# Self-attention stage with float16 value weights, DMA-placed low parts and one interleaved order for all units

## The reference

```python
xn = layernorm(x)
q, k, v = (einsum('ntc,hdc->nhtd', xn, w) for w in (w_q, w_k, w_v))
a = einsum('nhtd,nhsd->nhts', q, k) / 8
a = where(col > row, -inf, a)              # causal
y = einsum('nhts,nhsd->nthd', softmax(a), v)
x = x + y.reshape(8, 512, 1024) @ w_o
```

## Time and profile before

| what | value |
|---|---|
| median of 3 runs | 2338.05 us (2337.87 to 2339.3) |
| profiled execution, its own time | 2323.5 us |
| its span, first to last instruction | 2321.0 us |
| busy over the span: array, VectorE, ScalarE, GpSimd | 1981.3, 1371.9, 1193.5, 697.6 us |
| self-attention stage in the span | from the start to about 1023 us |

### The profile page before, as it was taken

The page is one execution under the profiler, slowest core; times in us unless marked ns, Lnnn a source line. Parts: engine busy times, 40 slices in busy tenths (PEclk is TensorE's granted clock), DMA queues, the critical chain, the costliest instruction groups (busy, mean ns, idle before and its releaser), DMA issues. The chain is left out here.

```text
span 2321.0 us, 38463 instructions
## 1 busy us (share of the span) xinstructions
PE 1981.3 (85%) x13976; PEld 1030.2 (44%) x13976; DVE 1371.9 (59%) x2614; ACT 1193.5 (51%) x2157; POOL 697.6 (30%) x691
## 2 busy tenths in 40 slices
PE   5899999999999999967999999957888888459983
PEld 2556565656665656542333332312333333236652
DVE  5564646465646464526787777835677876513354
ACT  2554545454545454533777777753555664125541
POOL 2110102011111010122333333114466666402266
PEclk8999999999999999987999999987999998779997
DMA  5111111110211111113323232200011201133355
GB/s 154 46 38 36 38 37 37 37 37 22 46 26 37 38 37 38 37 33 60 55 54 55 48 54 56 47 18 28 1 37 37 61 31 37 37 99 103 105 158 160
DMA packets 97081, 122.84 MB, mean 53 GB/s; under 512 B 14305, under 2 KB 73985, under 8 KB 96897
## 3 DMA queue, kind: packets, MB, share of 16 engines
q1 hardware_dynamic: 79872, 93.11, 17.1%
q0 software_dynamic: 6144, 16.79, 2.3%
q10 hardware_dynamic: 10880, 10.49, 1.3%
HBM read 52.64 MB, written 33.82 MB: 37 GB/s over the span
## 5 line engine op out<-in xcount | busy, mean ns | idle before, releaser
L1031 DVE TENSOR_REDUCE x_NM<-x_pm 128x1 f32<-128x512 f32 x512 | 342.4, 687 | 104.7 <-PE x_pm L774 102.5
L956 ACT ACTIVATE x_PR<-x_pS 128x512 f32<-128x512 f32 x512 | 300.9, 601 | 111.2 <-PE x_pS L790 104.4
L309 PE MATMUL a_pa<-a_PR,a_V 128*128 128x512 f32 (+3 forms) x1024 | 349.9, 449 | 0.7 <-ACT a_PR L389 0.3
L389 ACT ACTIVATE a_PR<-a_pS 128x384 f32<-128x384 f32 (+1 forms) x384 | 201.5, 525 | 220.8 <-PE a_pS L298 218.4
L469 DVE TENSOR_REDUCE a_NM<-a_pm 128x1 f32<-128x128 f32 (+3 forms) x512 | 233.6, 487 | 123.5 <-PE a_pm L284 120.2
L542 POOL CAST a_YT_hi<-a_Y 128x512 f16<-128x512 f32 x64 | 40.1, 626 | 773.2 <-DVE a_Y L477 773.2
L774 PE MATMUL x_pm<-x_KT,x_QT 48*128 48x512 f16 x512 | 195.9, 401 | 25.0 <-DMA x_QT<-q_k_parts 24.3
L790 PE MATMUL x_pS<-x_QT,x_KT 49*128 49x512 f16 x512 | 191.5, 390 | 17.9 <-ACT x_PR L956 16.3
L477 DVE TENSOR_TENSOR a_Y<-a_pa,a_RS 64x512 f32<-64x512 f32 x128 | 88.1, 688 | 182.1 <-ACT a_RS L397 180.0
L309 PEld LDWEIGHTS a_pa<-a_PR,a_V 128*128 128x128 f32 x1024 | 168.3, 191 | 36.8 <-ACT a_PR L389 11.7
L282 PE MATMUL a_pm<-a_KA,a_QA 128*128 128x128 f16 (+3 forms) x512 | 144.2, 308 | 31.2 <-DMA a_KB<-a_nat_k 17.0
(11 more groups left out here) (359 smaller groups left out, 4602.2 us busy)
## 6 DMA issues: line engine op xcount, KB each, us to landing
a_QA<-a_nat_q SPq DMA_DIRECT2D x128, 128.0 KB, 2.3
e_xr<-sent SPq DMA_DIRECT2D x80, 128.0 KB, 2.0
made<-e_eo ACTq DMA_DIRECT2D x40, 256.0 KB
a_KA<-a_nat_k SPq DMA_DIRECT2D x64, 128.0 KB, 2.3
a_KB<-a_nat_k SPq DMA_DIRECT2D x64, 128.0 KB, 2.4
x_KT<-q_k_parts SPq DMA_DIRECT2D x48, 128.0 KB, 4.8
x_QT<-q_k_parts SPq DMA_DIRECT2D x48, 128.0 KB, 4.5
f_w_stage<-in_w SPq DMA_DIRECT2D x12, 512.0 KB, 3.7
```

What stands on the lines that cost most here:

```text
L309: m = eng.matmul(pa[j % 2][:, P * kc:T], V[:, u % 2, kc, j, :], PR[:, i % 4, at:at + T - P * kc], start=(kc == 0), stop=(kc == TT - 1))
L389: eng.activation(PR[:, i % 4, 0:n], pS[i % 2][:, 0:n], ACT.Exp, scale=SCALE).then_inc(s_e, 1)
L956: eng.activation(PR[:, kc, j, :], pS[i % 2][:, :], ACT.Exp, scale=SCALE).then_inc(s_e, 1)
L1031: eng.tensor_reduce(NM[:, v % 2, c:c + 1], ring_bank("max", v, n)[:, :], AX.X, ALU.max, negate=True).then_inc(s_red, 1)
```

## The change

- Weighted values: the exponential is taken twice by ScalarE, once to float32 `PR` and once to a float16 `P16[0]`; GpSimd subtracts the two into `P16[1]`. Values are kept as float16 high and low parts. The array makes three float16 products where it made one float32 product. The exponent is lifted by a constant, `LIFT`, placed with the maxima.
- Low parts: VectorE writes one instruction of 128 partitions for each projection into a second `nat`, and SyncE places them. A unit has 12 copies instead of 8, and they wait for all four low parts too.
- Maxima: the mask product on the array is gone. VectorE adds a constant causal tile and reduces in one `tensor_tensor_reduce`, which writes its sum back to the bank.
- Output projection: in quarters of 128 rows, one with each unit from unit 5 on, and four behind the last unit. It uses one bank.
- Reciprocals: one exponential of 128 partitions for each pair of heads.
- Order: each engine merges its threads by written keys (`PLACE`, shifted by `TURN` for each unit) with `side_by_side`. A key orders instructions of one engine; nothing waits for a time. Three weight buffers instead of four; GpSimd presets its tiles ahead of the first norm.

```diff
+    TURN = 27.0
+    PLACE = {
+        ("PE", "QK"): (0, 1.079, 4.665, 5.819),
+        ("PE", "V"): (16.616, 18.25),
+        ("PE", "WO"): (22.355, 23.269),
+        ("PE", "MX"): (17.25, 17.251, 20.658, 20.767, 22.223, 23.127, 23.137, 23.929, 26.254, 27.724, 27.824, 27.978, 28.033, 28.408, 29.822, 31.85),
+        ("PE", "NM"): (35.785,),
+        ("PE", "S"): (42.27, 42.277, 44.705, 47.526, 48.721, 48.732, 53.428, 54.813, 55.471, 59.472, 64.864, 66.648),
+        ("PE", "AV"): (48.438, 48.446, 51.419, 54.507, 54.841, 54.993, 65.934, 67.354, 67.361, 67.363, 69.283, 70.389),
+        ("ACT", "QK"): (0.536, 4.995, 7.729, 12.911),
+        ("ACT", "NM"): (38.623,),
+        ("ACT", "E"): (43.172, 45.501, 48.258, 48.708, 48.729, 52.865, 54.31, 55.462, 59.26, 64.269, 67.143, 69.144),
+        ("ACT", "EX"): (57.744, 73.746),
+        ("DVE", "QK"): (1.902, 5.813, 14.352, 14.356),
+        ("DVE", "MX"): (18.872, 19.417, 20.855, 21.285, 22.224, 23.922, 24.781, 27.06, 27.157, 27.725, 27.825, 27.979, 28.034, 31.842, 35.775,
+            35.779),
+        ("DVE", "Y"): (65.794, 66.795, 73.747, 73.748),
+        ("SP", "CP"): (15.501,),
+        ("SP", "NP"): (42.262,),
...
+    FIRST = {"ST": -16, "RS": -13, "XN": -11, "XH": -7.5, "XL": -6}
+    TURNED = {"PE": (-1.6, -0.006), "DVE": (-1.0, -0.004)}
...
-            eng.matmul(o, QA[:, par, side, pair, t * P:(t + 1) * P], KA[:, par, side, pair, 0:(t + 1) * P],
-                       start=True, stop=False)
-            eng.matmul(pm[i % 2][:, t * P:(t + 1) * P], k.idb[:, :], k.mask_qk[:, :],
-                       start=False, stop=True).then_inc(s_mx, 1)
...
+                if i == 0:
+                    eng.wait_ge(s_cp[par], CPS * (u // 2 + 1))
+                    after(eng, s_ne, u)
+                after(eng, s_red, 16 * u + i - 1)
+                eng.matmul(pm[i % 2][:, 0:(t + 1) * P], QA[:, par, side, pair, t * P:(t + 1) * P],
+                           KA[:, par, side, pair, 0:(t + 1) * P], start=True, stop=True).then_inc(s_mx, 1)
...
+                for kc, a in SLOTS[sl]:
+                    for n, (v, p) in enumerate(((0, 0), (1, 0), (0, 1))):
+                        m = eng.matmul(pa[j % 2][:, P * kc:T], V[v][:, u % 2, kc, j, :], P16[p][:, i % RH, a:a + T - P * kc],
+                                       start=(kc == 0 and n == 0), stop=(kc == TT - 1 and n == 2))
...
+        side_by_side(over(weighted_values), over(scores), over(scores_for_max), over(projections, NU + 5))
...
+                eng.activation(PR[:, m % RF, 0:n], pS[i % 2][:, 0:n], ACT.Exp, scale=SCALE).then_inc(s_e, 1)
+                yield at("ACT", "H", u, i)
+                after(eng, s_av, m + 1 - RH)
+                eng.activation(P16[0][:, m % RH, 0:n], pS[i % 2][:, 0:n], ACT.Exp, scale=SCALE).then_inc(s_eh, 1)
...
+                eng.scalar_tensor_tensor(out=nat[1][qk][:, pair, :], in0=pp[c % 2][:, :], scalar=1 / WS,
+                                         in1=nat[0][qk][:, pair, :], op0=ALU.mult, op1=ALU.subtract).then_inc(s_lo, 1)
...
+                eng.tensor_tensor_reduce(out=pm[i % 2][:, 0:n], in0=pm[i % 2][:, 0:n], in1=causal[:, T - n:T], scale=1.0,
+                                         scalar=NEG, op0=ALU.add, op1=ALU.max, accum_out=NM[:, column(i)]).then_inc(s_red, 1)
...
+                eng.tensor_tensor(P16[1][:, m % RH, 0:n], PR[:, m % RF, 0:n], P16[0][:, m % RH, 0:n],
+                                  ALU.subtract).then_inc(s_el, 1)
...
+            yield at("SP", "CP", u)
             eng.wait_ge(s_hi, 4 * u + 4)
+            eng.wait_ge(s_lo, 4 * u + 4)
             after(eng, s_s, US * (u - 1))
...
+            for side, own in enumerate(sides):
+                for rows in sides:
+                    eng.dma_start(QA[rows, par, side, :, :], nat[0][0][own, :, :]).then_inc(s_cp[par], 16)
+                eng.dma_start(KA[own, par, side, :, :], nat[0][1][own, :, :]).then_inc(s_cp[par], 16)
+                eng.dma_start(KA[sides[1 - side], par, side, :, :], nat[1][1][own, :, :]).then_inc(s_cp[par], 16)
+                eng.dma_start(QB[own, par, side, :, :], nat[1][0][own, :, :]).then_inc(s_cp[par], 16)
+                eng.dma_start(KB[own, par, side, :, :], nat[0][1][own, :, :]).then_inc(s_cp[par], 16)
```

More of the change, by code:

```diff
@@ L192, in self_attention @@
     s_wo, s_xr = sem("wo"), sem("xres")
-    s_pre, s_pz = sem("presets"), sem("preset_parts")
+    s_pre, s_pz, s_causal = sem("presets"), sem("preset_parts"), sem("causal")
     SLOTS = [[(0, 0)], [(1, 0)], [(2, 0), (3, T // 2)]]
     NS = len(SLOTS)
-    NPRE = 2 * GH + 4
+    NPRE = 4 * GH + 4
     US = GH * NS
[L199 to L221, removed]
+    CPS = 12 * 16
     def slot_width(sl):
@@ L243, in project_qk, with over, transpose_x @@
+    def over(thread, n=NU):
+        for i in range(n):
+            yield from thread(i)
+    def tensor_program(eng):
+        def transpose_x(b, half):
+            eng.wait_ge((s_xhi, s_xlo)[half], b + 1)
+            if half == 0:
+                after(eng, s_vlo, 2 * NG * b)
+            else:
+                after(eng, s_xr, NG * b - 5)
+            turned(eng, pp[1 - half], xn16[half], k).then_inc(s_xt, 1)
         def project_qk(u, c):
             b, g = u // NG, u % NG
+            if u < NG and c == 0:
+                eng.wait_ge(weights.split_done, 2 * u + 1)
@@ L287, in scores @@
[L287 to L311, removed]
@@ new lines, in projections @@
+        def projections(u):
+            b, g = u // NG, u % NG
+            if g == 0 and u < NU:
+                for h in range(2):
+                    yield at_turned("PE", b, h)
+                    transpose_x(b, h)
+            for c in range(4 if u < NU else 0):
+                yield at("PE", "QK", u, c)
+                project_qk(u, c)
+            for h in range(2 if u < NU else 0):
+                yield at("PE", "V", u, h)
+                project_v(u, h)
+            if u >= 5:
+                yield from project_out(u)
@@ L429, in vector_program, with split_weights @@
+        def split_weights():
+            for n in range(NW):
+                yield at_split(n)
+                weights.high(eng, n)
+        eng.preload_act_table_set("natural_log_exp_and_others")
+        side_by_side(over(reciprocals), over(exponentials), over(maxima_out), over(projections), over(x_high, B), split_weights())
     def vector_program(eng):
         def statistics(b):
+            if b < 2:
+                eng.wait_ge(s_x[b], 16)
             for t in range(TT):
@@ L479, in residual, with x_out @@
[L479 to L484 removed]
+        def x_out(b, half):
+            eng.wait_ge(s_xt, 2 * b + half + 1)
+            if half == 0:
+                after(eng, s_v, 2 * NG * b)
+            eng.tensor_copy(xT[half][:, :, :], turned_view(pp[1 - half])).then_inc(s_xe, 1)
```

570 lines of the change are left out of this document (272 added, 298 removed).

## The result

The changed kernel is slower: 2436.03 us (2418.74 to 2437.75) against 2337.96, a ratio of 1.041, with a 95% interval from 1.036 to 1.046. I had forecast +47 us; it is +98. The sign and the mechanism hold. The size is off by a factor of two, and most of the miss is one term of the sum, the array's clock behind the pause.

The account below looks back on a forecast made before the run. The array was fullest before; after, a closed loop through SyncE's twelve copies was to set 32.0 us a turn. Turns summed to 976 against 939.3 us (+37), tail +10: 2338 + 47 = 2385 us, range 2335 to 2430.

Parts of the forecast that it names:

- The sign and the mechanism: Whole kernel: slower, chance 0.83, because the array stands still each turn while MX0 waits for SyncE's twelve copies.
- The closed loop: MX0 to QK3, then twelve copies on SyncE, then the next MX0: 30.3 us a turn, array idle about 5.6.
- The clock: Array at 1.2 GHz behind each turn's pause: between nothing and 1.6 us a turn, half taken, 0.8.
- The rest of a full turn: Loop of 30.3 us plus 0.9 for the new sequence every fourth unit, before the clock term: 31.2 us.
- Turns without a quarter: Four early turns, before output quarters begin at unit 5: 29.4 us each, 117 us together.
- The ends: First turn, without back part and paced by VectorE, 26.6 us; tail after the last unit's first copy 64.9 us, +10.
- Costs of the other engines: Per unit, ScalarE about 20 us, GpSimd 16, VectorE some 17: none fills 25 us, so their work is hidden.
- The rival of the slow reduction: VectorE's fused reduction at 1.7 times the plain one, +5.3 us a turn, partly in slack: 2425 to 2450 us, chance 0.1.
- The array as the bound: Rival: copies arrive within 6.4 us of QK3, so the array sets a 26.4 us turn: about 2210 us, chance 0.06.
- The Trainium skill's price of a DMA: Fixed 2.0 us and 436 GB/s: a unit's 1.5 MB of copies takes 5.6 us if they overlap freely.

Follow-up runs that it names:

- The better order: Changed kernel with MX0 waiting for only the eight QA and KA copies, maxima later in the array's order, and statistics later on VectorE: 2195.27 us, ratio 0.941.

## Why the prediction was right in sign and wrong in size

- **The closed loop: right, shown.** MX0 waits for the copies in every turn, 5.5 us where 5.6 was worked out. Twelve copies take 7.0 us (forecast 7.1), QK3 to the first 2.1 (2.1), the last landing 2.5 (2.8). Cutting the path at the wait (eight of twelve) and lengthening it in the kernel before (twelve of twelve) moved the time in the forecast direction, each by more than the copies themselves.
- **The clock: the step that failed.** "If none pays it is nothing, if all pay 1.6; I take half, 0.8." All 24 turns from 100 to 900 us paid (counted in the clock record), 2.4 us each in the mean, and with the pause filled a full turn fell from 33.2 to 31.1 us. So the term was worth 2.2 to 2.4 us and not 0.8. Two things were wrong in it. The 1.6 was read off one stretch behind the 3.97 us pause, where the low rate lasted from 1011.07 to 1014.19, and used as a ceiling for a pause of 5.6 us; behind the pauses of 5.0 to 6.7 us it lasted 3.3 to 6.0. Halving it had no row behind it at all. The Trainium skill (TensorE: Matmul & The Clock Gate, HAM oscillation) describes a loop that falls to half rate in each pass for such a wait. The trace agrees, in 24 turns of 24, and I had priced even that rule at 1.6.
- **The rest of a full turn: right.** The sum without the clock was 31.2 us. With the clock held at 1.00 by the spare products it measured 31.1.
- **Turns without a quarter.** Forecast 29.4, measured 32.95 each ((188.40 - 56.59) / 4): +14 us over four. With the pause filled the same four take 31.4 each, where the forecast without its clock term is 28.6, so 11 of the 14 us aren't the clock. I subtracted the quarter's 2.64 us, but VectorE still splits weights in these turns, as below, and the maxima wait behind it (0.34 and 0.97 us at 106.09 and 107.41). Such waits sum to 5.3 us from 58 to 188 us; from 191 to 900 us there is none. The other half of the 11 isn't split further.

```profile
101.88 2.17 DVE L121 SCALAR_TENSOR_TENSOR a_wo_lo<-a_w_stage,a_wo_hi 128x1024 f16<-128x1024 f32 x1
103.98 0.55 DVE L594 CUSTOM_DVE_ANT_0 a_pm<-a_pm,a_causal 128x384 f32<-128x384 f32 x1
```

- **The ends.** First turn 26.9 (26.6 forecast), tail 68.9 (64.9): +4 us. The terms add up: 26 x 1.2 + 14 + 0.3 + 4 is 50 us, on 47 forecast, against 98 measured. By cause: the loop's 31 turns take 1022.5 us with the pause and 959.7 with it filled, so the clock costs 63 us where 24 were forecast, 39 of the 50; the early turns are 11 more, the tail 4, and the full turns at full rate are 4 us short of the forecast.
- **Costs of the other engines: right where it mattered.** Subtraction of 384 columns 0.92 us (0.91 taken), low values 0.42 (0.42).
- **The rival of the slow reduction gave the right time for the wrong cause.** It would have come out at 2425 to 2450. By form, 100 to 900 us:

```profile
L594 DVE CUSTOM_DVE_ANT_0 a_pm<-a_pm,a_causal 128x512 f32<-128x512 f32 x96 | 67.7, 705 | 10.5 <-PE a_pm L424 8.6
...
L594 DVE DVE_READ_ACCUMULATOR2_ANT a_NM<- 128x1 f32 x384 | 54.3, 141 | 0.0
```

  It is 508 ns in the mean and 141 for a read of the accumulator that I hadn't counted, 0.65 us against the 0.487 taken, or 2.6 us a turn. With the mask back on the array the kernel was no faster, and the array hardly waited for these reductions, so this is hidden.
- **The array as the bound**, the rival at 2210 us, lost because twelve copies hold the queue for 7 us. The better order, with a wait for eight of them, shows that its number was near: a turn of 25.9 us in the mean where the rival had 26.4.
- **The Trainium skill's price of a DMA** (DMA: Bandwidth & Descriptors, Anatomy of one DMA) is a fit for single transfers that GpSimd issues, and I used it as if SyncE's twelve copies were one transfer. That estimate was 5.6 us; these rows show 9.5 us from the first issue to the wait's end. For one copy of 128 KB the same fit gives an estimate of 2.3 us, and the trace has a median of 2.3 (L676, issue to landing). What the estimate left out is the queue, which starts each copy only 0.64 us after the one before it.

## What to carry to other kernels

When a queue's transfers lie on a closed loop, find the pause that they leave the array, and price the slow stretch behind it from pauses of that length, several of them, or bound it wide; one stretch behind a shorter pause is no ceiling. Then ask which of the transfers the first reader needs and what work could stand between: here that turned a loss of 4% into a gain of 6% with the same arithmetic. Saved array time is worth next to nothing until the array is the bound, so measure such a saving in the order in which it will be used.

## What the runs showed of the hardware

- Behind a pause the array can run at its lower level, 1.2 GHz, for several microseconds. Behind pauses of 5.0 to 6.7 us in the changed kernel it always did (24 of 24), for 3.3 to 6.0 us, 4.9 in the mean. With pauses of 3.0 us in the mean it did so behind 16 of 24 (2.4 us over all), with 2.6 (the kernel before with spare copies) behind 14 of 24 (1.9 us), with 0.8 (spare products in the pause) behind none. The mean clock from 100 to 900 us was 0.90, 0.96, 0.97 and 1.00.
- So a wait can cost more than its length: 2.6 us off the path gave 3.9 us a turn.
- Copies of 128 KB issued one behind another on SyncE's queue start 0.64 us apart, and each lands 2.3 to 2.4 us after its own issue in the median (L676, L680). Twelve took 9.5 us until the array went on.
- The reduction with a second operand takes 705 ns for 512 columns, close to VectorE's scaling at 688, and each one is followed by an accumulator read of 141 ns.
- Normalizing 256 columns on VectorE (L545 after, L443 before) took 866 ns in the mean, 408 before. The trace shows what differs: four in a row took 1.38 us while GpSimd stood still, and 3.49 us while it worked beside them.

```profile
12.80 1.38 DVE L545 TENSOR_SCALAR a_xn<-x_res,a_mv,a_rstd 128x256 f32<-128x256 f32 x4 [5.58 <-POOL a_rstd L622]
...
122.15 1.84 POOL L635 TENSOR_TENSOR a_P_lo<-a_PR,a_P_hi 128x384 f16<-128x384 f32 x2 [1.12 <-ACT a_P_hi L503]
122.50 3.49 DVE L545 TENSOR_SCALAR a_xn<-x_res,a_mv,a_rstd 128x256 f32<-128x256 f32 x4
123.94 0.67 POOL L644 CAST a_YT_hi<-a_Y 128x512 f16<-128x512 f32 x1
```

  So it is throughout: the 28 that overlap a GpSimd instruction took 694 to 1316 ns, the other four 404 to 411, and all 32 of the kernel before, with GpSimd idle beside them, 403 to 414. Without the subtraction on GpSimd (the float32 values in the changed order) 25 of 32 are back at 398 to 411 ns, and the seven that still overlap took 820 to 828. Not every VectorE instruction is slowed: of the low parts (L572) the 60 that lie beside GpSimd's work took no longer than the rest, 685 to 692 ns in the mean, and the statistics (L531) 411 ns beside it and 413 without. What decides it isn't tested.
